# Making the low halves of the attention weights on TensorE instead of GpSimd, and issuing the first rows ahead of the constants

## The reference

```
K = 2 * einsum('chn,hnl->chl', B * C / (1 - dtA/2) * dt, exp(log(dA) * l)).real     # 8 x 256 x 512
h = concatenate([K, txt], axis=1)                                                   # 8 x 384 x 512
h = h + attention(layernorm(h), Wq, Wk, Wv, Wo)      # 16 heads, 4 key/value heads of 32, rotary
h = h + experts(layernorm(h), ...)                   # 64 experts, 6 per token, and a shared one
```

## Time and profile before

| | us |
|---|---|
| median of 3 runs | 1493.5 (1493.2 to 1501.09) |
| the profiled execution | 1496.6 |
| its span | 1494.8 |
| TensorE busy | 1286.1 (86%) |
| VectorE busy | 762.9 (51%) |
| GpSimd busy | 513.5 (34%) |
| ScalarE busy | 407.2 (27%) |

### The profile page before, as it was taken

How to read it: one execution, slowest core, us unless ns; L and a number is a source line. 1 busy time by engine, 2 the same in 40 slices (tenths; PEclk the granted TensorE clock), 3 DMA queues, 4 the chain that set the end, 5 groups by cost and what they waited for, 6 DMA issues and landing times. The chain is left out here.

```text
span 1494.8 us, 23215 instructions
## 1 busy us (share of the span) xinstructions
PE 1286.1 (86%) x9072; PEld 813.2 (54%) x9072; DVE 762.9 (51%) x1666; ACT 407.2 (27%) x670; POOL 513.5 (34%) x463
## 2 busy tenths in 40 slices
PE   4088469899899998989887969999999999989995
PEld 3088325354546464645443769666666656646662
DVE  7995366657676767686755462322232322322321
ACT  3111123333425343444434341111111111111110
POOL 3000101010303434253456357143344444434444
PEclk7589659799999899999988989999999999999998
DMA  3013241230514242422333355699999999989983
GB/s 111 0 46 78 56 101 34 61 69 12 151 27 130 61 125 65 118 71 74 95 85 142 124 196 148 162 303 288 352 307 322 322 332 329 293 277 306 324 278 40
DMA packets 139828, 239.80 MB, mean 160 GB/s; under 512 B 61112, under 2 KB 81224, under 8 KB 139720
## 3 DMA queue, kind: packets, MB, share of 16 engines
q1 hardware_dynamic: 115880, 214.10, 44.9%
q0 software_dynamic: 23840, 24.23, 9.2%
HBM read 175.59 MB, written 38.90 MB: 143 GB/s over the span
## 5 line engine op out<-in xcount | busy, mean ns | idle before, releaser
L1950 POOL DMA_INDIRECT out_rows<-mo_y,mo_scatter_half x128 | 181.1, 1415 | 248.5 <-DMA out_rows<-mo_y,mo_scatter_half 176.0
L1314 DVE TENSOR_REDUCE late_view<-at_ps 128x1 f32<-128x384 f32 x384 | 195.6, 552 | 79.6 <-PE at_ps L885 72.4
L1090 ACT ACTIVATE bulk<-at_ps 128x1152 f32<-128x1152 f32 x128 | 144.5, 1129 | 290.8 <-PE at_ps L851 274.5
L1573 POOL DMA_INDIRECT slot_table<-at_toki,at_si x144 | 143.7, 998 | 111.1 <-DVE late_view L1314 77.8
L70 PE MATMUL mo_ps<-arena_view,arena_view 128*117 128x384 f32 (+1 forms) x864 | 168.8, 344 | 1.1 <-PEq L541 1.1
L70 PEld LDWEIGHTS mo_ps<-arena_view,arena_view 128*117 128x117 f32 (+1 forms) x864 | 146.5, 179 | 14.6 <-issue 14.5
L885 PE MATMUL at_ps<-late_view 32*128 32x384 bf16 x384 | 101.7, 361 | 27.9 <-DVE late_view L1314 16.2
L842 PE MATMUL at_ps<-arena_view,arena_view 128*128 128x512 f32 (+1 forms) x576 | 115.1, 351 | 3.8 <-ACT arena_view L1168 2.3
L842 PEld LDWEIGHTS at_ps<-arena_view,arena_view 128*128 128x128 f32 x576 | 90.4, 193 | 37.2 <-issue 22.8
L851 PE MATMUL at_ps<-arena_view 97*128 97x384 f32 x384 | 100.4, 372 | 9.4 <-DMA arena_view<-late_view 5.1
L885 PEld LDWEIGHTS at_ps<-late_view 32*128 32x128 bf16 x384 | 27.7, 92 | 144.1 <-DVE late_view L1314 104.1
(11 more groups left out here) (210 smaller groups left out, 1809.2 us busy)
## 6 DMA issues: line engine op xcount, KB each, us to landing
bulk<-in_L_ffn_w_gate SPq DMA_DIRECT2D x32, 704.0 KB
bulk<-in_L_ffn_w_up SPq DMA_DIRECT2D x32, 704.0 KB
late_view<-in_L_ffn_w_gate SPq DMA_DIRECT2D x32, 704.0 KB
late_view<-in_L_ffn_w_up SPq DMA_DIRECT2D x32, 704.0 KB
arena_view<-arena_view SPq DMA_DIRECT2D x96, 192.0 KB
late_view<-in_L_ffn_w_down SPq DMA_DIRECT2D x32, 512.0 KB
bulk<-in_L_ffn_w_down SPq DMA_DIRECT2D x32, 512.0 KB
out_rows<-at_hr SPq DMA_DIRECT2D x8, 768.0 KB, 3.8
```

The source lines that it names most:

```text
L1090: A.activation(PT[:, N % RING, :, :], ps[:, 0:NT, 0:SEQ], ACT.Exp, scale=float(HD) ** -0.5)\
L1314: V.tensor_reduce(maxes[:, half, s, h:h + 1], ps[:, raw_bank(a, u), 0:SEQ], AX.X, ALU.max, negate=True)\
L1573: G.indirect_dma_start(slot_table, bass.IndirectOffsetOnAxis(ap=si[:, e % 2, m:m + 1], axis=0), toki[:, e % 2, m // TOPK:m // TOPK + 1], N ...
L1950: G.indirect_dma_start(acc_halves, bass.IndirectOffsetOnAxis(ap=scatter_half[:, half, 2 * p + e:2 * p + e + 1], axis=0), y[:, p % 2, e, co ...
```

## The change

Part one. GpSimd's list in the state-space phase goes, with the buffers `passing`. ScalarE first makes a negated identity, `minus_one`. For each block TensorE now also computes the low part itself, in a third PSUM bank: it multiplies the block with the identity in fp32 (which turns it once more) and adds to the same bank the negated identity times the high half. ScalarE copies the result to the low half. TensorE's order is: turn block n, then the leftovers of block n - 1. ScalarE's order is: high half of n, low half of n - 1.

Part two. In SP's queue of the attention phase the three transfers of rows of sequence 0 stand ahead of the seven constants and the two pads.

```diff
+        minus_one = part(arena, ARENA - P, [P], F32R)
-        psK = ps("ss_psK", [P, 2, 512])
+        psK = ps("ss_psK", [P, 3, 512])
+        def turned_bank(n):
+            return psK[:, n, :].rearrange("p (k o) -> p k o", k=KC)
...
-            act.wait_ge(e_read, 1)
+            nc.scalar.activation(minus_one, ident, ACT.Copy, scale=-1.0).then_inc(minus_ready, 1)
+
+            def weights_low(n):
+                act.wait_ge(w_left, n + 1)
+                nc.scalar.activation(halves(n)[1], turned_bank(2), ACT.Copy).then_inc(w_lo_done, 1)
+
             for n in range(NW):
-
-                if n >= 2:
-                    act.wait_ge(w_lo_done, n - 1)
                 act.wait_ge(w_turned, n + 1)
-                turned_block = psK[:, n % 2, :].rearrange("p (k o) -> p k o", k=KC)
-                nc.scalar.activation(passing[n % 2], turned_block, ACT.Copy).then_inc(w_passed, 1)
-                nc.scalar.activation(halves(n)[0], turned_block, ACT.Copy).then_inc(w_hi_done, 1)
+                nc.scalar.activation(halves(n)[0], turned_bank(n % 2), ACT.Copy).then_inc(w_hi_done, 1)
+                if n >= 1:
+                    weights_low(n - 1)
             act.wait_ge(w_turned, NW + 1)
...
+            weights_low(NW - 1)
...
-            dve.wait_ge(w_lo_done, NW)
...
-        @block.gpsimd
-        def _(pool):
-            G = nc.gpsimd
-            for n in range(NW):
-                pool.wait_ge(w_passed, n + 1)
-                pool.wait_ge(w_hi_done, n + 1)
-                hi, lo = halves(n)
-                G.tensor_tensor(lo, passing[n % 2], hi, ALU.subtract).then_inc(w_lo_done, 1)
-
...
+            pe.wait_ge(minus_ready, 1)
+
+            def weights_left(n):
+                pe.wait_ge(w_hi_done, n + 1)
+                wait(pe, w_lo_done, n)
+                for k in range(KC):
+                    ks = slice(k * P, (k + 1) * P)
+                    T.matmul(psK[:, 2, ks], rows[:, n, ks], ident, start=True, stop=False)
+                    m = T.matmul(psK[:, 2, ks], minus_one, halves(n)[0][:, k, :], start=False, stop=True)
+                m.then_inc(w_left, 1)
+
             for n in range(NW + 1):
-
-                if n >= 2:
-                    pe.wait_ge(w_hi_done, n - 1)
+                wait(pe, w_hi_done, n - 1)
...
                 m.then_inc(w_turned, 1)
+                if n >= 1:
+                    weights_left(n - 1)
             pe.wait_ge(w_hi_done, NW + 1)
+            pe.wait_ge(w_lo_done, NW)
...
         @block.sync
         def _(sp):
-            for dst, src in ((ident, ident_in), (cos, cos_in), (sin, sin_in), (upf, upper_in),
-                             (tokf[:], tok_in), (iota[:], slot_in[0]), (slot0[:], slot_in[1])):
-                sp.dma_start(dst, src).then_inc(consts_in, 16)
-            sp.wait_ge(ones_ok, 1)
-            sp.dma_start(xrow[B * SEQ:B * SEQ + CAP, :], x2_rows[0:CAP, 0, :]).then_inc(pads_in, 16)
-            sp.dma_start(acc[B * SEQ:B * SEQ + CAP, :], x2_rows[0:CAP, 0, 0:D]).then_inc(pads_in, 16)
-
...
             rows_in(xn, 0, a_in)
+            for dst, src in ((ident, ident_in), (cos, cos_in), (sin, sin_in), (upf, upper_in),
+                             (tokf[:], tok_in), (iota[:], slot_in[0]), (slot0[:], slot_in[1])):
+                sp.dma_start(dst, src).then_inc(consts_in, 16)
+            sp.wait_ge(ones_ok, 1)
+            sp.dma_start(xrow[B * SEQ:B * SEQ + CAP, :], x2_rows[0:CAP, 0, :]).then_inc(pads_in, 16)
+            sp.dma_start(acc[B * SEQ:B * SEQ + CAP, :], x2_rows[0:CAP, 0, 0:D]).then_inc(pads_in, 16)
+
```

More of the change, by code:

```diff
@@ L182, in state_space_phase @@
         factor = (Za[:, 0], Za[:, 1], minus_zi)
-        passing = [C[:].rearrange("p c s n r -> p (c s n r)")[:, j * KC * P:(j + 1) * KC * P]
-                   .rearrange("p (k o) -> p k o", k=KC) for j in range(2)]
+        minus_one = part(arena, ARENA - P, [P], F32R)
         def halves(n):
@@ L207, in state_space_phase @@
         w_turned = sem("ss_w_turned")
-        w_passed = sem("ss_w_passed")
+        w_left = sem("ss_w_left")
+        minus_ready = sem("ss_minus_ready")
         w_hi_done = sem("ss_w_hi_done")
```

## The result

The changed kernel takes 1477.16 us (median of 20 runs, 1467.57 to 1486.6). The kernel before, beside it, takes 1492.47 (20 runs, 1481.83 to 1501.09). The ratio is 0.9913, with a 95% interval from 0.9891 to 0.9936: 13.0 us less, between 9.6 and 16.3. The direction was forecast.

The account below looks back on a forecast made before the run. The prediction took VectorE's chain from 17 to 81 us, slowed by GpSimd's subtractions, to bound the product's start. Gains of 7.2 and 3.2 us sum to 10.4: 1493.5 - 10.4 = 1483.1 us, range 1480.5 to 1490.5.

Parts of the forecast that it names:

- What bounds the begin: From 17 to 81 us VectorE is the busy engine; each microsecond it loses should move the state-space product's start.
- VectorE's gain, 7.2 us: VectorE's chain to 81.02 us without GpSimd's subtractions: long operations save 1.40, copies 1.8, two squarings 4.0; together 7.2 us.
- The new work at nothing: 80 TensorE products in the weight chain cost nothing: they end at 48, ScalarE is free at 49, cover about 10 us.
- 58.8 allowed: Moment in us by which ScalarE must be free, so its squares are ready for VectorE's L388.
- the rows that stood in: Other TensorE work pricing the new products: 256-column records at 0.138 us each, transposes of 128 columns at 0.131.
- The rival of a low clock: Clock stays low in the weight chain; ScalarE free at 61.2, VectorE stalls 2.4 us; 1485.5 us; chance 0.1.
- the slow one: Weight chain: fp32r product costs as much as fp32, clock stays at 1.2 GHz; stall 14.0, time 1497.1 us; chance 0.05.
- The rows, 3.2 us: Begin of attention: rows issued ahead of constants, last constant lands at 154.4 us, statistics start 3.2 us earlier.
- 0.1 to 0.2 allowed: Begin of attention: microseconds added to the last constant's landing for sharing with the rows' data.
- 0.8 for the carry: Allowance at the low end of the range for the shift's passage through later stages, beside 7.6 + 4.6 = 12.2 us.
- its rival for the carry: Attention's half-clock stretches keep the shift from reaching the end; with 4 us lost, 1487 us; chance 0.15.
- The last of its signs of being wrong: Span from first statistics to the end differing by more than 3 us from 1337.2.

Follow-up runs that it names:

- idle subtractions: Changed kernel cut behind the state-space phase, plus ten GpSimd subtractions on a scratch area nobody waits for before 70 us: 155.47 us.
- the kernel without low parts: Kernel before, cut behind the state-space phase, without GpSimd's subtractions or new TensorE products; ScalarE's unrounded copy goes to the low half: 147.34 us.
- the cut changed kernel: Changed kernel without attention and experts, one transfer writing the tokens of sequence 0 to the output: 147.17 us.
- part two alone: Kernel before, GpSimd's subtractions kept, with only the three transfers of rows moved ahead of the constants: ratio 1.0021 whole; 938.61 us without the experts phase.
- the pair without experts: Kernel before and changed kernel, each without its experts phase: 941.38 and 929.59 us.
- the cut kernels: For the 11.8 us shift: kernel before and changed kernel, both cut behind attention, without the experts phase: 941.38 and 929.59 us.
- the cut kernel before: Kernel before without attention and experts, one transfer writing the tokens of sequence 0 to the output: 155.36 us.

## Why the prediction was right and where it was wrong

**What bounds the begin.** Right. VectorE's chain is what starts the product, and GpSimd's presence beside it was the delay. The idle subtractions give the delay back and the kernel without low parts doesn't have it.

**VectorE's gain, 7.2 us.** It measured 81.02 - 73.65 = 7.4 in the first pair of profiles. The two copies take 0.28 us from their start to that of their successor, less than the 0.50 allowed, the long pair 2.40 instead of 2.50, and two squarings 2.11, as forecast.

**The new work at nothing.** Right, with 147.17 against 147.34 us. ScalarE was free at 42.6 us, where 49 were forecast and 58.8 allowed. The price of a block was over-estimated: 1.37 us against 1.63, 0.114 for a record where the rows that stood in gave 0.138 and 0.131. The clock rose at about 20 us, not 26 (after 22 in the trace of the cut changed kernel). The rival of a low clock didn't come about, nor did the slow one; against the 58.8 of the prediction the weight chain could have lasted 16 us longer.

**The rows, 3.2 us.** The trace has 10.57 - 6.94 = 3.6. The last constant was issued 4.95 us after the first row, not the 5.3 of the forecast, and landed 1.99 us later, against 1.93 before. So behind the rows it lost 0.06 us, less than the 0.1 to 0.2 allowed: it is late because it is issued late. When a second queue issues it earlier, its transfer takes longer, 3.7 us, and it lands no earlier. The trace of part two alone has 3.0 us, and the whole time of that kernel couldn't show it.

**What was left out.** The sum had no term for the product's own length. It takes 61.0 us in the profile before and 61.7 after, as its clock rises later after its start (at 78 us, 4.4 us after it, against 83.9, 2.9 us). In the pair without experts it is 63.9 before and 61.2 after, with pauses of TensorE in the first. It is worth a few microseconds in either direction, whichever kernel runs.

**The step that failed** is in "How the numbers follow": the term of the range for what happens behind the change, "0.8 for the carry". The prediction took a shift of the start to pass through the rest whole, and its rival for the carry gave a price only to a loss (1487). The last of its signs of being wrong came about. From the first statistics to the end the two profiles differ by 1337.2 - 1324.95 = 12.3 us, and not by at most 3. As shown above, 9.3 of these lie between the first and the last sum of attention and 4.7 behind it. The kernel before takes 494.7 us instead of 510.1 between these sums in another execution, and the part behind them scatters by 12 us from trace to trace. So no run shows this excess to be the change's work.

Put in the terms of the sum: the shift is 11.8 us by the cut kernels, against 10.4 forecast. Both of its terms were sized a little low, 7.4 to 7.6 for 7.2 and 3.6 for 3.2, and the rest, under a microsecond, lies within the scatter of the product. That alone would give 1493.5 - 11.8 = 1481.7, inside the range. Of the other 4.5 us down to 1477.16, 1.0 is the base: the kernel before came to 1492.47 over 20 runs, where the forecast started from 1493.5 of three. The last 3.5 are the difference between the medians, 15.3, and the shift. They belong to no edit that was tested. The ratio's interval, 9.6 to 16.3 us, holds both the forecast 10.4 and the 11.8. So the mechanism of the change was right, and a range for the absolute time should have allowed for some 4 us more of scatter at either end.

**What stays open** is what makes the later stages of one and the same program vary: attention in the first two profiles (510.1 and 500.8 us, against 492.5 to 496.7 in nine others) and the experts phase in all. In the profile before TensorE's granted share was lower in attention, 0.94 against 0.97, but the one after had 0.97 like the others. It is also open why the kernel before stood some microseconds too near to the others in one set of runs and too far in another, and what TensorE's pauses in the product are. None of this was tried further.

## What to carry to other kernels

When an engine is slow only beside another one, look at the operands and not only at semaphores: here VectorE's operations with two inputs in SBUF waited for GpSimd's subtractions, which read SBUF, and not for its fills, though neither engine depended on the other. Work that moves from GpSimd to an idle TensorE can cost nothing even if one instruction becomes eight, as long as its last result is due late enough. And terms of some 3 us in a kernel that scatters by 20 are measured by cutting the program behind the stage, or read at a landmark of the trace, not from the whole time.

## What the runs showed of the hardware

The turning of blocks held the full clock by itself. In the cut kernel without low parts, where TensorE has only transposes from 17 to 28 us, its row for 17 to 36 us has a granted share of 0.90 with TensorE busy 9.21 us of 19; in the profile before the same transposes ran at 0.50 throughout. Its source line of the transposes' loads (min/median/max ns):

```profile
L448 PEld LDWEIGHTS ss_psK<-ss_ident,bulk x40: 138/141/231, 17.8 to 27.8; 128*128 128x128 f32 x40
```

The loads take 141 ns in the median, against 230 at half clock in the profile before. There the clock had already fallen before these transposes began, here it hadn't.

Transposes alone also raised it. In the trace of the cut kernel before the share had fallen to 0.50 by 16.5 us. TensorE then had nothing but transposes, without a pause from 16.84 to 19.66 us, and the slices from 20 to 26 us are at 1.00. Its stages and the same loads:

```profile
17.00:24.00 7.00, 4.82 (x26) 3.71 (x27) 5.95 (x6) 4.26 (x9) 3.83 (x4) 0.80 0.00 0
24.00:30.00 6.00, 2.70 (x14) 1.82 (x14) 5.96 (x6) 3.62 (x7) 5.96 (x4) 0.72 0.00 0
L459 PEld LDWEIGHTS ss_psK<-ss_ident,bulk x40: 137/164/230, 17.5 to 31.2; 128*128 128x128 f32 x40
```

It fell again in the slice from 26 to 27 us, while TensorE waited 1.55 us for ScalarE. The Trainium skill, "TensorE: Matmul & The Clock Gate", section "Part 4: PE-mode transpose", says that the full clock doesn't engage for transposes. These two traces don't bear that out, neither for keeping it nor for reaching it, if the fp32 transposes of this kernel are what the page means. So in one kernel the turning can run at either level from one execution to the next, and VectorE's chain ends at 81.0 to 81.3 us with both.

The share needs a second look beside it. In the trace of the kernel before without experts it stands at 1.00 from 17 to 36 us, while the loads of the transposes take 230 ns in the median, as at half clock. The durations of the loads are the safer guide.
